# One attention and FFN block on one core: the written orders of all five engines and the PSUM banks of its units are replaced by others

## The reference

```python
x = x + _layernorm(_L0_attn_ref(_layernorm(x), qkv_w, qkv_b, proj_w, proj_b))
x = x + _layernorm(_L0_ffn_ref(_layernorm(x), U1, V1, b1, U2, V2, b2))
# attention: 16 heads of 16, rotary q and k, causal softmax
scores = einsum('bhid,bhjd->bhij', q, k) * scale;  attn = softmax(where(causal, -inf, scores))
out = einsum('bhij,bhjd->bhid', attn, v) @ proj_w.T + proj_b
# FFN: 256 -> 64 -> 1024 -> gelu -> 64 -> 256
einsum(gelu(einsum(einsum(x, U1), V1) + b1), U2), V2) + b2
```

## Time and profile before

| | |
|---|---|
| median of 3 runs | 1206.49 us (1203.6 to 1208.54) |
| profiled execution | 1208.03 us, span 1206.3 us |
| busy | PE 96%, PEld 51%, DVE 78%, ACT 78%, POOL 55% |
| instructions | 25813 |
| mean granted TensorE clock | 0.992 of full speed |

### The profile page before, as it was taken

One profiled execution on the slowest core, in us unless ns is written; L12 is line 12 of the kernel. 1 busy time (PEld: TensorE's weight loads), 2 busy tenths in 40 slices (PEclk: granted clock), 3 DMA queues, 4 the chain that ended last, 5 costly groups with the idle time before them and its releaser, 6 DMA issues.

```text
span 1206.3 us, 25813 instructions
## 1 busy us (share of the span) xinstructions
PE 1155.2 (96%) x9844; PEld 619.4 (51%) x9844; DVE 941.1 (78%) x1458; ACT 941.8 (78%) x1898; POOL 658.8 (55%) x718
## 2 busy tenths in 40 slices
PE   5899999999999999999999999999999999999995
PEld 4655446544654456445654564455545554454542
DVE  6998786789678886888678958896888886476666
ACT  4477878788868877887878877887788689678785
POOL 2467325944495349633874387346844343336647
PEclk9899999999999999999999999999999999999998
DMA  6586544665555745576367636762766443402413
GB/s 202 180 143 127 106 66 79 159 130 103 111 140 132 133 81 142 128 107 140 93 147 104 144 81 152 115 151 37 177 117 127 100 96 114 131 1 92 154 54 122
DMA packets 99259, 142.22 MB, mean 118 GB/s; under 512 B 24896, under 2 KB 60992, under 8 KB 99136
## 3 DMA queue, kind: packets, MB, share of 16 engines
q1 hardware_dynamic: 99136, 140.58, 51.9%
HBM read 79.70 MB, written 51.38 MB: 109 GB/s over the span
## 4 chain that ended last, share of the span: by engine, by line
PE 63%; DMA 9%; SPq 8%; DVE 8%; POOL 7%; ACT 3%; issue 2%; DVEq 0%; POOLq 0%; ACTq 0%
PE PV L875 16%; PE RING L857 12%; PE RING L822 10%; PE RING L776 6%; DMA QK<-split_parts 4%; PE RING L886 3%; PE RING L789 3%; PE RING L927 3%; SPq L649 3%; PE RING L920 3%; SPq L624 2%; DVE MB L1015 2%; PE RING L828 2%; DMA X<-x 2%; ACT PB L1206 2%
## 5 line engine op out<-in xcount | busy, mean ns | idle before, releaser
L1206 ACT ACTIVATE PB<-RING 128x512 f32<-128x512 f32 (+2 forms) x1280 | 623.5, 566 | 139.4 <-PE RING L857 130.9
L1015 DVE TENSOR_REDUCE MB<-RING 128x2 f32<-128x1024 f32 (+2 forms) x448 | 497.0, 1142 | 96.1 <-PE RING L828 48.1
L857 PE MATMUL RING<-QK 64*128 64x512 f32 (+3 forms) x1536 | 320.5, 395 | 1.5 <-DMA QK<-NSROW 0.9
L1301 POOL TENSOR_SCALAR_AFFINE_SELECT PB<-PB 128x512 f32<-128x512 f32 x256 | 160.9, 638 | 275.1 <-ACT PB L1206 274.7
L822 PE MATMUL RING<-QK 62*128 62x512 f32 (+3 forms) x1536 | 296.2, 387 | 14.2 <-DMA QK<-split_parts 8.7
L857 PEld LDWEIGHTS RING<-QK 64*128 64x128 f32 x1536 | 169.2, 186 | 156.1 <-ACT PB L1206 92.3
L1015 DVE TENSOR_REDUCE M<-RING 128x2 f32<-128x768 f32 (+1 forms) x186 | 191.3, 1041 | 56.1 <-PE RING L828 55.3
L875 PE MATMUL PV<-PB,VL 128*32 128x512 f32 (+3 forms) x2048 | 224.1, 522 | 0.5
L822 PEld LDWEIGHTS RING<-QK 62*128 62x128 f32 x1536 | 156.7, 186 | 126.8 <-DVE MB L1015 36.3
L828 PE MATMUL RING<-MASKK,MASKQ 64*128 64x128 bf16 (+1 forms) x768 | 112.5, 248 | 0.0
L1231 ACT ACTIVATE F_H<-RING,F_B 128x512 f32<-128x512 f32 x128 | 80.5, 687 | 18.6 <-PE RING L920 18.5
(11 more groups left out here) (141 smaller groups left out, 1507.8 us busy)
## 6 DMA issues: line engine op xcount, KB each, us to landing
QK<-split_parts SPq DMA_DIRECT2D x372, 128.0 KB, 5.8
split_parts<-PARTS SPq DMA_DIRECT2D x60, 256.0 KB, 3.1
split_parts<-EO SPq DMA_DIRECT2D x60, 256.0 KB, 3.6
ATT<-OT SPq DMA_DIRECT2D x128, 64.0 KB
INV<-inverse_sums SPq DMA_DIRECT2D x32, 256.0 KB
block_mid<-Y SPq DMA_DIRECT2D x16, 512.0 KB, 4.4
F_X<-block_mid SPq DMA_DIRECT2D x16, 512.0 KB, 5.6
out<-F_Y SPq DMA_DIRECT2D x32, 256.0 KB, 2.1
```

The lines of the kernel that those rows point to most:

```text
L857: ins = e.matmul(m[:, i, :], QK[g % 3][r, 1, k, 128 * j:128 * j + 128], QK[g % 3][r, 0, k, 512 * c + off:512 * c + 512], start=True, stop= ...
L1015: e.tensor_reduce(acc, ring(("max", g, s, u), pairs, n), AX.X, ALU.max).then_inc(v_max, 1)
L1206: e.activation(buf[:, h, pairs[0]:pairs[-1] + 1, :], strip(("score", g, s, u), pairs, n), ACT.Exp).then_inc(a_exp, 1)
L1301: e.affine_select(buf[:, :, 0:128], buf[:, :, 0:128], pattern=[[0, 4], [1, 128]], base=0, channel_multiplier=-1, compare_op=ALU.is_ge, fil ...
```

## The change

Only the strings of `ORDERS` and `PLACES` differ. Each kind of step occurs as often as before on each engine, but for `heat`, a matmul on zeros: two before, one after. So TensorE has 2813 steps before and 2812 after. Of the steps, 694 of 1864 on ScalarE, 493 of 1057 on VectorE, 216 of 528 on GpSimd and 110 of 272 on SyncE stand at another position, most by one or two. On TensorE 285 keep their position and 2119 are off by one; the farthest is off by 11. Of 2243 units with banks, 688 have other ones. Of each string the beginning is shown; the rest is changed in the same manner.

```diff
--- before.py
+++ after.py
@@ -153,106 +153,106 @@
     "PE": (
-        "HxxqqqqqqqqvvvvxxfqqqqqqqvqvvvxmmxmmmmqvFqqvhhmmqmmmqqmssqmssmqmsmsmvmvmsmxptmsmmsmxmssmpsmpmsssmsspssmsmq"
-        "ssmqmssmmsspmsssmpmssmmsmmpsmmtpsssmssqqmssmpssmqmmssqsmpssmppsssmssqqssmmppmsssmsmsspssmsmpssmsspmsmtssmp"
...
+        "HxxqqqqqqqqvvvvxxfqqqqqqqvqvvvxxmmmmmmhvqFvqqmmqmmmqqmsssmqmmssqmmmsmvvmxptmmsssmmmxmsspmspmsssmsspsmssmqs"
+        "smqmssmssmpmmssspmmsmpsssmmpsmstmsmssqqmssmpssmqmssmqmsspmsppsssmssqqmssmppmsssmsmsspssmsmpssmsspmsmsstmps"
...
     "ACT": (
-        "llllwxxqqlllqqrlxxvrqqqllqrllxrvvxvFlqvqqeeleleelqreexteveelexeeeeeeeeeeeqeoleeeeeereeeteeeeeeeeqleeeqeeee"
...
+        "llllwxxqllqlqqrlxxrqqlvqqrvlllxrvvxFvqqleeqlelleeqrevxteeexeeeeeeeeeeeleeoqeeeereeeeeeeelteeeeeeqeeeeqeeee"
...
     "DVE": (
-        "ssssdqxxswsssdssrrsrrlrxxrsdslrrrrrlrxsflmsmmsxmdmsmssXsdssmmmmmmmmmmmmmmaxbmmmmmmxmmmmmmmmmmmmmmmammbmmmm"
...
+        "ssssdqxxssssdwssssrrrrlrxxrdsslrrrrrlrxslfmmmxsdmmmXssssdssmmmmmmmmmmmmmmaxbmmmmmmmxmmmmmmmmmmmmmsmammbmmm"
...
     "POOL": (
-        "pppoporrrslpsrsrsrlsssrrssrsslsrrrlsssssssssssssssspssssssssarrarrrrlssssalsssarrrslrrrlssssPsssssPRsssRss"
...
+        "poppprrrslosrssprrlsrssssrrsrslsrrlssssssssssssssspsssssssassrrrarlrrsssslassasrrrslrrrlssssPsssssPsRsRssR"
...
     "SP": (
-        "xssffssffHgshgashgsaahsgaahgaamhoabmgohbsasgshasagaahgxaamhtoatbmgohbsasghssaagahagxtaamhamobghtobssgashsa"
...
+        "xssffssffHgshgahsgashsagahagaamhobamgohbssgashasagaahgxatahmgaotmbohbssgahssaagaahgxaamhotbgamobhatssgshsa"
...
 PLACES = (
-        "0120304506120304602301534123456012356125612340561203412563415613405612356431245634012534601263412056340560"
...
+        "0120304056123562340563412563412056034125634120563412345601235623014564230156340125601342561034156103124035"
...
```

More of the change, by code:

```diff
@@ L161 @@
[L161 to L165, removed]
@@ new lines @@
+        "pmsssspmsmssppmsssmpsmssmspsssmmpssssmtpsmssmspssmsspmmssppmssvvmssmvvmssssxpsmsssxssmpppmssmqqssmmpssmqqs"
+        "smmqqssssmvvvqqvmssmtpjmssmjpjssssmjmsssspmmsspxsssmspxppssssmqqqqmmsspqmssmqmssppssmsmqqmsmsspjmssssjmpss"
+        "ssmtjjssmmpssmppsssssmpssssmpssmsssppmmsspssmsssmpmsmssppsmsspssmsspmsmsspssmsmssmsstpmmmspsmmssspssmsmssp"
+        "msssmpssmspmmssspssmppmsmsspsmssmspsmsmsssspsmmsstpsmssmspssmsspsssmppmmssvvvmssmvssmpsmssssxssmpppxmssssp"
+        "qssssmqqqssmmpssmqvqssmqqvssmmvvssmtjpmssmjjjssmmpmssxpssmsspxmssssppmqmmqqqssmmsqqssmsspppsmmssqqssssmjpm"
@@ new lines @@
+        "mssjsssmtpsmssmpssmmjssmpmsssspjmsssspmsspsmsmssppssmspsssmpssmsspmssmsspssmmsspssmpmsssspmsstmsmmpsssmpms"
+        "ssmssmpsssmppmsmsspmssssspsmsmssppmmssspmsssmpmsmssssspmsssstpsmssmpsmssmpssmppssmvvmssmvvmssxmsssspssmmpp"
+        "ssmpxsspmmssqqqmssssqqssmpssssmqqqmssmvvvvtmmssppjjssssmjjmssmpxmsssspppmssxpmssssqqmmssqqmmssqqqmmsspqmss"
+        "sspmmjssmpjssmsspmssmpssssmtpmssmpjssssmjmsspmsssmpsmsspsmsspmsssmpssmsspsmssppssmsspmmsspmssspmsssspmtsms"
+        "msspmssmpssmsmsspsmssmspsmsspmmsppssmssmspmsmsspsmsssspsmssmsmssmpsssstmspssmsmspmsssmpppssmvvmssmvvmssssp"
@@ new lines @@
+        "mmsspxssssmppmxmsspmssmqqqqqqssssmvvssqqssmmpssssmvvtssmjjssmpppmssmjjssmssmxmsspppmssmxsssspmmssqqqqmssmq"
+        "msspppssmmqqqssmmspssmssjtssmjjssmmjssmpssssmpmssmpmsspmsssssppmsmsspsssmsmspsmmssspssppmssmpsmssmsssssmss"
+        "ptsssmpsmssmpssmsmpssmsmsspsmssmppsssmpmssmsssmspmsssmppmsmsspsmsssspmmsssmptsssmpsssssmpmmsspssmppmmssvvm"
+        "sssspmmssvvmssxmsspsmssppssmxpssssmqqsssmqqmmsspmssmvqvqqqmssmvvssmtpssssmxxjjppssmpmssssjpjpssssmqqmssssp"
+        "mmqqqqqmssqmssmpssmppmssjssmssjssmsspmmsspmssmtpmmpsssmmjssmjssssmpssmpsmsssspmsmspsmsspssmpsssssmppmssmss"
@@ new lines @@
+        "sspsssmpmssmspssmmtpsmssmpmsmsspsssmpsmssmpmssspmsmsspsssmpsmsmsspsmsssmsmsspssmmpsssssmptssmpsssssmpmmppp"
+        "ssssmvmsmvsssvmmssvmssxmssppmssmppxmsspmssssvvqqssmqqssssmqqmssmqqssssmvvpptssmmjjmssmxjjpmmssxpmsssspppms"
+        "sssqqmsssspmmssqqmssppmssmqqmssmqqssssmpjmmssjssmptssssmpmmjssmjssmmmppmssspmssmspssmpssmspsmssspmssssppms"
+        "spmssspssmsspssssmspmsssssmtpmssmpmmsspmsssmssmspsmsspsmssmspmssspmmsssppsmmssspmsssmpsmssmmsssstpsssmpsss"
+        "smpmmsspssmppssmvssmmvmsspmsssvssssmvmsmpppssmmjjssssmjssmjmsssspmmsspmssmpsssmmtpmmssspjmssssjmsspppmsssm"
@@ L183 @@
+        "psssmjssmssjmmsspsmssppsmsssmsssspsmsmsmmsspsmssmtpssmmpmsspssmmpsmsspsmsspmssssspsssmmpssssppmmspssspsmsm"
+        "sspmsmsssstsssspssTsspTssssspssppsTsssspssssspppTsssspsspsssssUsssssppsssssTssppuuppTuuddduuTjjTuudddUddTu"
+        "uTjjuuTjjTuuUddjjuuyTuuTduuyuTdddddTuyuuUddddTuuyTuuTddddTuudUdduuyuTdddTuuyuTdduuTyuuddddddUddTuuTuyuuTdd"
+        "TuuUuyuuTddTuuyuTddTuuddUdduuyuddddyuudduuyddddduuydddyy"
     ),
     "ACT": (
-        "llllwxxqqlllqqrlxxvrqqqllqrllxrvvxvFlqvqqeeleleelqreexteveelexeeeeeeeeeeeqeoleeeeeereeeteeeeeeeeqleeeqeeee"
@@ new lines @@
+        "eeeoeeeeeteeeereeeeeeeeeeeeeeeeoeeyeeeeeeeeeoeeeyeeeeeeeeeeyeeeteyeyyeyeeeeeeeeyeeeoeeeeeeeeoeeeeeeeeeeeee"
+        "eeteeeeeeeeeeeellelelvoeeveeeeeeeeexoxeeeeeeeqeeqeeeeelqqveellvreeteleeeeexreeeexeeeeqqeeoeqeeeeeeeqeeeere"
+        "oeeteeeeereeeeeeeeeyeeeeeeeeeoeeeeeeeeeeeeeeeoeeeyeeyeeeeeteeyyeyeeyeeeeeeeeoyeeeeeeeeeeeeoeeeeeeeeeeeeete"
+        "eeeeeeeelleleeelveeoveeeeeeeexeeoxeeeeqleeeqeeeleleeqeqeevvletereeeeerexeeeeoeexeeeeqeeqyeeqeeqeeeereeoeee"
+        "eeeeetereeeyeeeeeeeeeeeeeeeoeeeeeeeeeeoeeeyeeeyeeeeeeeteyeeeyyeyeeeeeeeeeeoeeeeeeeeeoeeeeeeeeeeeeeeeteeeee"
@@ new lines @@
+        "eeeeeeeoelvlleeeeeelveexeeeeoxeeeqeqqeeeleveeeeqeeeetevleerleelereeeeexeoeexeeeeeeqqeeeeeeqoqeeeeeeetreeee"
+        "eereeeeeeeeeeeeeeeeeeoeeeeeyeeeoeeeeeeeeeeeeteeeeyyeeeyeyeeeeeeeyeeeoeeeyeeeyeeeeeeoeeeeeeeeeeeteeeeeeeeee"
+        "eeoeleveeeelleelveexeeeeeoeexeeeeqeeeqleleeeqvlqeelvteeeeerxxeeereeeeeoeeeeeeqqeqeeeeqeeeoeeeeeeeeereeeter"
+        "eeeeeyeeeeeeeeeeeeeoyeeeeeeeeeeeoeeeeeeeeeeeyeteyeeyyeeyeeeeeeeeoeeeyeeeeeeeeeeeeeeoeeeeeeeeeteeeeeleeelee"
+        "eeoelveeeleeveexeeeeoxeeeeeveeqelqeeeeqeelqleveeetreeleexexereeeeeeeeoqeeeeeeqeeeeqeeqeeeereoeeeteeeeeeree"
@@ new lines @@
+        "eeeeeyeeeeeeoeeeeeeeeyeoeeeeeeeeeeeeeeeteeyeeeeeyeeeeeeeeeeoeeeyeeeyeeeeoeeeeeeeeeeeteeeeyeeeeeeeeeeeoeeev"
+        "eeeeeeeeyveoeeeeeeeeeeeeeeeeeteeeeeeeeeeeoeeeeeeyyeeeeeeeeeoeeeeeeeeeeyeeeyeyteeyeeyyeeeeeeeeeeoeeeeeeeeee"
+        "oeeeeeeeeeeeeeteeeeeeTeeeeTeeeeeeeoeeeeeTeeeeoeeeeeeeTeeeeeeeeeeeeeeeeeTggggoggTgggTgggggggTTgTggggQgTggTg"
+        "gggggggTgggTgggngynTgggyQTggygggnyngTggggTgnnTggygQgTggyygngggTngggggTgggTgQggggygngnTnnggQTggggggTnTggggT"
+        "nggggggggTnggTggnTgggggTQgggnnggngggngggggQngnngggnggggnnQnnnn"
@@ new lines @@
+        "mmmmmmmmmmmmmmsmammbmmmmmmmmmmmdmmmmmmabmmmmmmmmmmmmmmmmmmmmambmmmimmmmmmmxxmmmmmmmmmammbmmipmpmmmSmxxmmmm"
+        "mmmmSmSmmSpmambpDmmmmmmSmmmmmmmSSmmmmmaSDmbmmmmmmmmmmmmmmmmmmmssssammbdmsmsmssmidmmmmmmmxxmmimmmmmmambmmpp"
+        "mSmmmxxmmmmSmmmmmmSmmapbmSmmDmmmmmmpmmSmSmmmmmmSmmSaDmbmmmmmmmmmmmmmmmmmmmsssamsbdimsmsmmmsmsmmmdmmmxmxmmi"
+        "mmmmmammbpmpmmmxSSmxSmSDmmmmmmmmmmpmmmambmmmpmmmmmmmSmSmSmSmmDmmambmmmmmmmmmmmmmmmmmmsmambsmsmmmsdmmmmmimm"
+        "xmmmxssssidmmmmmmambpmmmpmmmxmmxSmSmmmmmmmmmabmpSmmmpSmmmmmmmmDmmmSSmmmmmaSSDbmmmmmmmmmmmmmmmmmmmmamsbmsss"
@@ L215 @@
+        "dmimmmmmsmmmmixmmmsxsmsdmmmmmmammbmxxpmmpmmmSmSSmmmmmSDmmmpmambmmmmmmpmmmmmSmmSSmmmmmSmaDmbmmmmmmmmmmmmmmm"
+        "mmmmssssamdbmsismmmsmsmmmmmxmmmdmxmmmimmambmmpmmxpmmmxmmSmmSmmmSmmSmmmDpammmbmmpmmmmmmmmSmmmSSmSDmmmambmmm"
+        "mmmmmmmmmmmmmmmmamibmmmmmmmmmmmmmmmpmimmpmmmmSambmmmmSSmpSDmmmmpmmmmSSmSSmmDmmambmmmmmmmmmmmmmFmmmmabRFRFW"
+        "RUiFRFRFpRiUFpSSRFSpUSpYYPRSDFYSYRFRSPSUDYYPYYPFRUFYRYPYYPFYYRFPURYYPFURFYYPRYYPUYYYPYPYYPYYPYYYPYPNNAA"
     ),
     "POOL": (
-        "pppoporrrslpsrsrsrlsssrrssrsslsrrrlsssssssssssssssspssssssssarrarrrrlssssalsssarrrslrrrlssssPsssssPRsssRss"
@@ L222 @@
+        "sRssspssssspssarrarrrrsslsslassarssrrrrrllsPsssssssPssRsRssRssRssspssssssaparrrsrrarslssaslssPsrrrrlrrlsss"
+        "sssssPRsssRsRssssRsssspssssprrraasrrrlssslssassarrrrrrllssssssPsssPssssRsRssRRsssspssassparrrrrssrlsslassa"
+        "srsrrrrrllPsssssssssPsRsRsssRsRsspsssaassssprrrrrlrsssslsassasrrrrlrrlsPsssssssssPsssssRssRssssasssaRsaaRs"
+        "sssPsssPRRssRRssssssfssfssssssfssfssafaffaafFPAfAfFPAFAFAAfRfARAFfFARAFAfRAFfAfAAFAAFAAAFFAAAFAFAAAAFFAA"
     ),
     "SP": (
-        "xssffssffHgshgashgsaahsgaahgaamhoabmgohbsasgshasagaahgxaamhtoatbmgohbsasghssaagahagxtaamhamobghtobssgashsa"
@@ L225 @@
[L225 to L226 removed]
+        "xssffssffHgshgahsgashsagahagaamhobamgohbssgashasagaahgxatahmgaotmbohbssgahssaagaahgxaamhotbgamobhatssgshsa"
+        "agaahgxaatmhgamotobhabssghassaghaagaxamhoabmtgobhsstaghssaagaahgaxamhobttagmhobsasgshasagaahgaamohbtgamobh"
+        "tagahaLaahIaatmobRamotbSSSNSSSNSStStSNSSSSSSSSSSSSSSSSSSSSSS"
     ),
@@ new lines @@
+        "6301243560123015634015621034560134210563421034562015612340534601201234561234563412056340125340125630561234"
```

(21 more changed lines are left out.)

83 lines of the change are left out of this document (6 added, 77 removed).

## The result

The changed kernel takes 1212.74 us (median of 20 runs, 1207.05 to 1219.74), the kernel before 1206.44 beside it (20 runs): a ratio of 1.0054, 95% interval 1.0038 to 1.0070. So it is 6.3 us slower, where I had forecast 2.5 faster, with 1209 as the end of the range. The profiled execution took 1210.02 us, 2.7 under its median; that of before, 1208.03 us, stood 1.6 above its own.

The account below looks back on a forecast made before the run. TensorE, 96% busy, was taken to bound the middle, the SP and DMA chain the start. Terms of -0.36, -0.24, -0.4, -0.45 and -1.0 summed to -2.45 us, forecasting 1204.0 us against the median 1206.49; range 1196 to 1209.

Parts of the forecast that it names:

- item 7: Last part: f_y and three downs replace four downs after the last up; tail order same; nothing, 0.3 us at most.
- Rival C: In the middle, closer bank reuse makes TensorE wait and delays emptying on VectorE: slower, 1214 us; chance 0.08.
- Items 1 to 3 and 5: TensorE changes of split -0.36, score-strip slots -0.24, borders after masked maxima -0.4 us; one heat matmul fewer before group 1, nothing.
- Item 4: Opening: new DVE order around the first rotation and last remainder shifts SP's queue of sends and loads: -0.45 us.
- Item 6: Reuse of banks by maxima and scores at changed distances alters TensorE's waits: -1.0 us, bounds -3.3 and +7.9.
- rivals B: Hidden waits for banks shrink throughout, one in fourteen closed: 1199.4 us; chance 0.28.
- rival D: TensorE's saved changes are absorbed by waits for banks, only the opening counts: 1206.0 us; chance 0.13.
- Rival E: Opening: a second half-clock spell of 10.24 us would cost 5.1 us at most: 1209 us; chance 0.04.

Follow-up runs that it names:

- old front with new tail: Old orders and bank places up to score(30,10,1), about 1003 us, the changed kernel's from there on: 1214.85 us, ratio 1.0069 to the kernel before.
- light adds: GpSimd's residual adds cut to one column of 256: in the changed kernel 1204.51 us, ratio 0.9987; in the kernel before 1204.01 us, ratio 0.9974.
- pow: Changed kernel with one-column residual adds, a GpSimd pow over 128x4 ahead of each: 1205.36 us, ratio 0.9983 to the kernel before.
- new front against before: Changed kernel's orders and bank places up to score(30,10,1), the old ones from there on, against the kernel before: 1208.10 us, ratio 1.0012.
- adds moved: Changed kernel, seven GpSimd adds moved away from f_rows(10) to (13): 1209.55 us, ratio 1.0009; same last part behind old orders up to score(30,10,1): 1208.84, 0.9991.
- no collisions in the old kernel: Kernel before, GpSimd adds in the last part moved so none runs beside f_rows(9), (12) and (14): 1219.26 us, ratio 1.0109.
- the first moves: Changed kernel with only three GpSimd adds moved, those beside f_rows(10) and (11): ratio 1.0030 to the kernel before.

## Why the prediction was wrong

The step that failed is item 7, "Last part", "Nothing, 0.3 at most". It looked at TensorE's order behind the last up and took the rest as unchanged, with the sentence above the list that "the durations of single instructions stay"; the description of the kernel says the same with "Nothing else sets the time". The durations don't stay: the last eight `f_rows` take 7.3 us more (14.7 and 22.0), and TensorE waits for VectorE there. Measured: T grew by 4.7 us between the two profiled kernels, and by 4.2 and 6.0 where the same fronts are compared (the 6.0, old front with new tail, holds a spell of 3.4 us at half the clock); in medians the new tail costs 0.42% (1.0054 against 1.0012) to 0.69%, 5 to 8 us. None of the rivals had it. Rival C had the sign and, as a side remark, VectorE as what gets late, but put it in the middle and on banks.

The same item says that the tail from the last down on stands in the same order. It does, and yet it takes 1.0 us more: the time from the last matmul to the end, "some 14 us", which "should stay", went from 14.3 to 15.3. The swap that item 7 costed is where this can come from: f_y(6,1) now starts 5.4 us ahead of f_y(7,1) instead of 7.0, and the adds of f_res(6) behind it 1.5 us later against the same mark, so that the last of them meets L1119. That this swap alone does it was not tested; that the adds do it is shown by the runs with light adds and with pow, where L1119 takes 0.17 us under the same order.

"Wrong would be a stretch of 50 us anywhere in the middle that gains or loses over 2 us by itself": such a stretch came, 1100 to 1150 us, only not in the middle.

Items 1 to 3 and 5, together -1.0, are below what the runs can tell. Three pairs compare new and old front with one tail: +0.12% (new front against before), -0.15% (the full change against old front, new tail) and +0.18% (adds moved), in the mean +0.05%, or 0.6 us, give or take some 1.6. So the -2.45 in all doesn't show. F says the same over 14 profiled executions: old fronts 1031.6, 1027.7, 1032.5, 1027.4, 1030.6 and 1028.4, in the mean 1029.7; new ones 1027.9, 1029.6, 1027.2, 1031.6, 1030.3, 1028.1, 1030.0 and 1027.7, in the mean 1029.1. The same front scatters by 5 us, and the two profiles that I compared first happened to lie 3.7 apart. Two of the high values (1032.5 and 1031.6 of the new ones) are of profiles with a spell of 3.4 us at half the clock near 770 us, as a wait for the load of a group ended. T scatters less: 159.3 and 159.8 for the old tail, 164.0 and 165.4 for the new one, 159.0 twice with all moves, 157.9 and 158.0 with light adds and 157.9 with pow.

Item 4, "the first maximum at about 42.9 to 43.0 instead of 43.38": it stands at 43.39.

```profile
43.39 0.69 PE L822 MATMUL RING<-QK 62*128 62x128 f32 x4 [1.25 <-DMA QK<-split_parts]
```

Over all profiled executions it is 43.0 in the mean with old fronts and 43.2 with new ones, and the first maximum of group 1 71.6 against 71.7. The 0.45 us isn't there. My reading of the rows was fine (the wait before it fell from 3.33 to 1.25 us, since a transpose now stands there), but the place of a step on SP's chain moves by more than that from one execution to the next.

Item 6, banks, -1.0 with bounds of -3.3 and +7.9: the waits for banks came out at 156.6 us over 290 places against 157.1 over 298, so neither the reuses counted as closer nor those counted as wider changed them, and no gain or loss of the front shows. A count of distances in the order string was no price here, and the value nearest to "what a hidden wait costs, nothing" would have been nothing. With the waits unchanged, the rivals B ("shrink throughout") and C fall by their own marks, a tenth less and 8 us more. For the front rival D, only the opening counts, comes nearest, without its opening.

Rival E: in the profile the clock fell once in the opening, as before, and for somewhat longer (the second fall, from some 1197 us on, lies behind the last matmul in both). The granted clock averages 0.51 over 40.25 to 53.85 us, against 0.50 over the 10.24 us in the earlier trace rows; half speed is 1.2 GHz. As group 1 starts no later for it, it cost nothing there.

```profile
40.25:53.85 13.60, 11.77 (x55) 8.31 (x56) 12.61 (x24) 3.64 (x7) 1.69 (x4) 0.51 0.76 231
```

One profile doesn't settle it, though. Of the 103 executions with the new front whose clock is on record, 14 had a mean granted clock of 0.985 or less, three of them of the full change (0.981 to 0.983, 1216 to 1220 us); of the 150 with the old front none did. The means are 0.9887 and 0.9904, and among the new fronts each 0.001 less goes with 0.93 us more, which makes an estimated 1.6 us in the mean. So a gain of that size from the items of the front may be there and be eaten by the clock; where in the run it falls, and why, no profile shows, for the 14 profiled executions have 0.987 to 0.992. The loss in the tail doesn't come from it: it stands in profiles at 0.990, and old front with new tail lost 8 us at 0.989 to 0.990.

## What to carry to other kernels

The duration of an instruction is a property of its neighbours too: where the shortest and longest of one line differ by a factor of three, as 0.4 and 1.38 us did for `f_rows` before, find what runs beside the long ones, and price a new order by how often it brings them together. An instruction moved out of such a collision is still waited for by others, above all by loads into the buffer that it frees; look at them first. And compare stretches over several profiled executions before believing a gain of a few us: here one stretch scattered by 5 us and another by 0.5 to 1.4, and a spell at half the clock in one profile was as large as the effect that was read from it.

## What the runs showed of the hardware

A GpSimd tensor_tensor of 128x512 (1.28 us) that reads and writes SBUF holds up a VectorE tensor_scalar of 128x256 in SBUF from 0.41 to 1.37 us, one instruction for each add, and one of 128x4 from 0.17 to 1.12; GpSimd itself loses little (1.28 to 1.33 us, at most 1.37). A pow over 128x4, 1.0 to 1.2 us of GpSimd, does nothing to either. VectorE's sums that read PSUM and bn_stats aren't held up: before, beside the add at 1111.62 us, they take 0.67 and 0.75 us (for two), as elsewhere.

```profile
1111.40 0.67 DVE L1101 TENSOR_TENSOR F_Y<-RING,F_B 128x512 f32<-128x512 f32 x1
1112.11 0.75 DVE L1105 BATCH_NORM_STATS2 F_YST<-F_Y 128x6 f32<-128x256 f32 x2
```

In the last part the granted clock fell to 0.50 as long waits of TensorE ended: for 6.8 us with a wait of 5.3 us and for 3.4 us with one of 3.8 (no collisions in the old kernel), and for 3.4 us with one of 2.1 (the first moves, and old front with new tail). The two spells near 770 us came with waits of 1.6 and 2.3 us for the load of a group. A wait of 2.0 us at F_P in the profile of the full change had no such spell.
